# Second buffer for the gathered expert rows, passed on by ScalarE; scatter indices copied by VectorE; one TensorE wait per producer

## What is computed

```
x = x + L0_xattn(ctx_1024, layernorm(x))            # alignment, 8 x 100 rows of 512
h = layernorm(x)                                    # 800 rows
raw_gate = softmax(h @ gate)                        # 16 experts
_, topk_idx = top_k(raw_gate, 3)                    # TOP_K = int(16 * 0.2) = 3
gate_topk = normalised raw_gate of the 3 chosen
hidden = relu(h @ W1[e] + b1[e])                    # 512 -> 1024
expert_out = hidden @ W2[e] + b2[e]                 # 1024 -> 512
x = x + sum_e gate_topk[e] * expert_out[e]
x = x + L1_xattn(...);  x = x + L1_ffn(...)         # not touched by the change
```

## Time and profile before

| | |
|---|---|
| median of 3 runs | 1178.19 us (1177.99 to 1180.57) |
| the profiled execution: its own time | 1184.01 us |
| the profiled execution: span | 1181.7 us |
| TensorE (PE) busy in the span | 1042.0 us, 88% |
| GpSimd (POOL) busy in the span | 275.0 us, 23% |
| mean granted TensorE clock | 0.95 of full speed |

### The profile page before, as it was taken

The page is one execution under the profiler, slowest core; times in us unless marked ns, Lnnn a source line. Parts: engine busy times, 40 slices in busy tenths (PEclk is TensorE's granted clock), DMA queues, the critical chain, the costliest instruction groups (busy, mean ns, idle before and its releaser), DMA issues. The chain is left out here.

```text
span 1181.7 us, 19755 instructions
## 1 busy us (share of the span) xinstructions
PE 1042.0 (88%) x6297; PEld 642.8 (54%) x6298; DVE 520.6 (44%) x1963; ACT 327.8 (28%) x854; POOL 275.0 (23%) x416
## 2 busy tenths in 40 slices
PE   8967579956968998999989999889999999999997
PEld 7962235533455555555556555565456655555553
DVE  6837887884672222222222222237865643121212
ACT  4624755771121111111111111234254420000000
POOL 1852021110002333333333333410030001121211
PEclk9977889977988999999999999989999999999999
DMA  8857005118515574767677565570030005000000
GB/s 321 241 126 248 1 0 176 65 55 207 205 38 183 156 223 146 230 196 248 177 248 248 174 204 151 178 207 0 1 143 1 2 1 160 1 1 0 14 14 28
DMA packets 74653, 148.28 MB, mean 125 GB/s; under 512 B 12930, under 2 KB 24970, under 8 KB 73758
## 3 DMA queue, kind: packets, MB, share of 16 engines
q1 hardware_dynamic: 63750, 129.11, 33.0%
q0 software_dynamic: 9520, 14.56, 6.1%
q10 hardware_dynamic: 1320, 3.84, 1.3%
HBM read 128.16 MB, written 19.33 MB: 125 GB/s over the span
## 5 line engine op out<-in xcount | busy, mean ns | idle before, releaser
L1412 ACT ACTIVATE att<-ba,b 128x64 f32<-128x64 f32 x180 | 41.7, 314 | 232.9 <-PE ba L1335 232.9
L1318 PE MATMUL ba<-shared,att 128*64 128x256 f32 x736 | 91.2, 391 | 0.0
L2536 PE MATMUL acc<-tiles 128*128 128x400 f32 x256 | 90.6, 505 | 0.0
L2602 DVE SCALAR_TENSOR_TENSOR tiles<-bf,shared 128x400 f32<-128x400 f32 x64 | 32.4, 568 | 129.9 <-PE bf L2521 129.6
L1318 PE MATMUL ba<-Wmem,att 128*64 128x256 f32 x672 | 84.6, 395 | 1.0 <-ACT att L1397 0.5
L1343 PE MATMUL ba<-shared,att 128*64 128x256 f32 x736 | 84.6, 383 | 0.3 <-ACT att L1412 0.3
L1343 PE MATMUL ba<-Wmem,att 128*64 128x256 f32 x704 | 79.7, 379 | 0.0
L1432 DVE TENSOR_TENSOR att<-ba,att 128x256 f32<-128x256 f32 x45 | 19.1, 425 | 135.8 <-PE ba L1343 135.8
L2495 PE MATMUL bf<-shared,Wmem 128*128 128x400 f32 x192 | 70.0, 501 | 2.3 <-PEq L53 1.6
L2536 PEld LDWEIGHTS acc<-tiles 128*128 128x128 f32 x256 | 47.1, 190 | 40.4 <-issue 8.6
L1427 DVE TENSOR_SCALAR att<-ba,b 128x64 f32<-128x64 f32 x180 | 38.7, 277 | 68.6 <-PE ba L1335 68.5
(11 more groups left out here) (412 smaller groups left out, 1881.6 us busy)
## 6 DMA issues: line engine op xcount, KB each, us to landing
Wmem<-in_W SPq DMA_DIRECT2D x16, 2048.0 KB, 9.2
shared<-in_W SPq DMA_DIRECT2D x16, 2048.0 KB, 9.1
cT<-in_ctxT SPq DMA_DIRECT2D x8, 1444.0 KB, 14.7
ctx_rows<-in_ctx SPq DMA_DIRECT2D x8, 1280.0 KB
Wmem<-in_Wkv SPq DMA_DIRECT2D x2, 2048.0 KB, 8.3
tiles<-in_WoT SPq DMA_DIRECT2D x4, 1024.0 KB
Wmem<-in_WiT SPq DMA_DIRECT2D x3, 1024.0 KB, 6.9
cost_mem<-dist SPq DMA_DIRECT2D x8, 330.6 KB, 5.0
```

The lines of the kernel that those rows point to most:

```text
L1318: ins = pe.matmul(pa[part][h * Q:(h + 1) * Q, :], xT[:, k, :], w[:, k, h * HH + part * DQ:h * HH + (part + 1) * DQ], start=k == 0, stop=k ...
L1412: act.activation(hT[:, j, :], pt[0][:, n * P + half * Q:n * P + (half + 1) * Q], ACT.Relu, bias=b1[:, bass.ds((e + u) * HJ + j, 1)]).then_ ...
L2536: ins = pe.matmul(acc[k][:, 0:NT4], WoT[:, f, k * P:(k + 1) * P], hs[i % 4][:, :], start=f == 0, stop=f == FJ - 1)
L2602: dve.scalar_tensor_tensor((h1[i % 4], h2[i % 2])[k][:, :], bank[i % NBK][:, 0:NT4], 0.0, wb[k][:, g * NT4:(g + 1) * NT4], ALU.max, ALU.mu ...
```

## The change

`res["xg_sb"]` is a buffer for gathered rows with two halves in each of its slots. One more half, `ahead`, is now the target of every gather from the third on, and ScalarE copies it on to `rows` (`pass_on`) once it has landed in `ahead` and once the rows before have been turned; the copy raises `rows_ok`. GpSimd's `gather(c)` waits for `rows_ok` in place of TensorE's transposes, and TensorE waits for `rows_ok` in place of the transfer. The gather of the third chunk's rows is issued in the routing stage, behind the two that were there. The scatter's indices are copied by VectorE (in `output`, between its two operations, after the wait for the earlier scatter) and no longer by GpSimd. In TensorE's program several waits are gone: `turn_hidden` waits only for `a_rd[1]`, the second half of `first_layer` for nothing, and `second_layer` once for each of `h_ok[0]` and `h_ok[1]` (until all four relus of ScalarE, or of VectorE, are done) where it waited for each relu by itself. Waits at the end of the stage that counted gathers are gone too.

```diff
--- before.py
+++ after.py
@@ -1014,8 +1014,8 @@
 
             pool.wait_ge(idx_ok, 1)
             pool.wait_ge(kept_rows, 32 * B)
-            for i in range(2):
-                pool.indirect_dma_start(out=res["xg_sb"][:, i, 0:DQ], out_offset=None, in_=half_rows(res["xn_d"]),
+            for i, to in enumerate((res["xg_sb"][:, 0, 0:DQ], res["xg_sb"][:, 1, 0:DQ], res["xg_sb"][:, 0, DQ:D])):
+                pool.indirect_dma_start(out=to, out_offset=None, in_=half_rows(res["xn_d"]),
                                         in_offset=bass.IndirectOffsetOnAxis(ap=res["gidx"][:, i:i + 1], axis=0)).then_inc(res["xg_in"][i], 16)
 
         @block.tensor
@@ -1243,7 +1243,7 @@
     raw, y_last, y_more = pieces[:, 2, 0:DQ], pieces[:, 2, DQ:D], pieces[:, 3, 0:DQ]
     b2 = [pieces[:, 4, u * DQ:(u + 1) * DQ] for u in range(2)]
     xT = pieces[:, 5, 0:KD * Q].rearrange("p (k s) -> p k s", s=Q)
-    first_rows, rows = xg[:, 0, 0:DQ], xg[:, 1, 0:DQ]
+    first_rows, rows, ahead = xg[:, 0, 0:DQ], xg[:, 1, 0:DQ], xg[:, 0, DQ:D]
     from_row, to_more, to_last = (sb(n, [P, 1], I32) for n in ("from_row", "to_more", "to_last"))
     pa = [bank[0][:, 0:DQ], bank[1][:, 0:DQ]]
     pt, px, py = bank[2:4], bank[4][:, 0:DQ], bank[5][:, 0:DQ]
@@ -1251,9 +1251,10 @@
     w1_in, w2_in, xg_in = res["w1_in"], res["w2_in"], res["xg_in"]
     b1_in, x_back = sem("b1_in"), res["x_back"]
     a_mm, a_rd, h_ok = ([sem(f"{n}{i}") for i in range(2)] for n in ("a_mm", "a_rd", "h_ok"))
+    rows_ok = sem("rows_ok")
     xt_mm, xt_ok, t_mm, y_mm, py_rd, y_ok = (sem(n) for n in ("xt_mm", "xt_okd", "t_mm_e", "y_mm", "py_rd", "y_ok"))
     last_out, more_out, zeros = sem("last_out"), sem("more_out"), sem("zeros_e")
-    from_ok, to_ok = sem("from_ok"), sem("to_ok")
+    from_ok = sem("from_ok")
     took = sem("took_e")
     first_chunk = res["table"]
 
@@ -1312,7 +1313,8 @@
 
     def expert_pe(pe):
         def first_layer(c, w, part):
-            pe.wait_ge(a_rd[part], c)
+            if part == 0:
+                pe.wait_ge(a_rd[0], c)
             for k in range(KD):
                 for h in range(2):
                     ins = pe.matmul(pa[part][h * Q:(h + 1) * Q, :], xT[:, k, :], w[:, k, h * HH + part * DQ:h * HH + (part + 1) * DQ],
@@ -1325,10 +1327,7 @@
             ins.then_inc(xt_mm, 1)
 
         def turn_hidden(c):
-            for part in range(2):
-                pe.wait_ge(a_rd[part], c)
-            pe.wait_ge(h_ok[0], JH * c)
-            pe.wait_ge(h_ok[1], JH * c)
+            pe.wait_ge(a_rd[1], c)
             for i in range(2):
                 for n in range(2):
                     q = 2 * i + n
@@ -1338,7 +1337,8 @@
         def second_layer(c, w):
             pe.wait_ge(py_rd, c)
             for i, n, half, j in turned:
-                pe.wait_ge(h_ok[i], JH * c + 2 * n + half + 1)
+                if n == 0 and half == 0:
+                    pe.wait_ge(h_ok[i], JH * c)
                 for h in range(2):
                     ins = pe.matmul(py[h * Q:(h + 1) * Q, :], hT[:, j, :], w[:, j, h * DQ:(h + 1) * DQ],
                                     start=j == 0, stop=j == HJ - 1)
@@ -1348,7 +1348,7 @@
             pe.wait_ge(xt_ok, c + 1)
             first_layer(c, w1, 0)
             turn_hidden(c)
-            pe.wait_ge(xg_in[1], 16 * c + 16)
+            pe.wait_ge(rows_ok, c)
             turn_rows(rows)
             first_layer(c, w1, 1)
             second_layer(c, w2)
@@ -1383,9 +1383,9 @@
         pe.wait_ge(w2_in[1], 24 * (E_N - 2) + 48)
         with pe.Fori(c0 + 1, c1) as c:
             step(c, W1[1], W2[1])
+        pe.wait_ge(a_rd[0], c1)
         turn_hidden(c1)
         second_layer(c1, W2[1])
-        pe.wait_ge(xg_in[1], 16 * c1 + 16)
         pe.sem_inc(xt_mm, 1)
         pe.sem_inc(a_mm[0], 1)
         pe.sem_inc(a_mm[1], 1)
@@ -1396,12 +1396,16 @@
             act.wait_ge(a_mm[1], c + 1)
             act.copy(xT.rearrange("p (h m) s -> p m h s", h=2), px.rearrange("p (m h s) -> p m h s", m=2, h=2)).then_inc(xt_ok, 1)
 
-        act.sem_inc(h_ok[0], JH)
+        def pass_on(c):
+            act.wait_ge(xg_in[2], 16 * c + 16)
+            act.copy(rows, ahead).then_inc(rows_ok, 1)
+
         act.wait_ge(xt_mm, 1)
         act.copy(xT.rearrange("p (h m) s -> p m h s", h=2), px.rearrange("p (m h s) -> p m h s", m=2, h=2)).then_inc(xt_ok, 1)
         act.wait_ge(a_mm[0], 1)
         act.copy(pre[:, 0:DQ], pa[0]).then_inc(a_rd[0], 1)
         keep_rows(0)
+        pass_on(0)
         act.wait_ge(b1_in, 16)
         with act.Fori(0, E_N - 1, 2) as e:
             for u in range(2):
@@ -1415,6 +1419,7 @@
                     act.wait_ge(a_mm[0], c + 1)
                     act.copy(pre[:, 0:DQ], pa[0]).then_inc(a_rd[0], 1)
                     keep_rows(c)
+                    pass_on(c)
 
     def expert_dve(dve):
         def keep_second(c):
@@ -1427,15 +1432,16 @@
                 dve.tensor_scalar(hT[:, j, :], pt[1][:, n * P + half * Q:n * P + (half + 1) * Q], b1[:, bass.ds(e * HJ + j, 1)], 0.0,
                                   ALU.add, ALU.max).then_inc(h_ok[1], 1)
 
-        def output(c, u, y, y_out, before):
+        def output(c, u, y, to_row, y_out, before):
             dve.wait_ge(y_mm, c)
             dve.tensor_tensor(raw, py, b2[u], ALU.add).then_inc(py_rd, 1)
+            dve.wait_ge(y_out, before)
+            dve.sem_inc(took, 1)
+            dve.tensor_copy(to_row[:, :], res["oidx"][:, bass.ds(c - 1, 1)])
             dve.wait_ge(py_rd, c + 1)
-            dve.wait_ge(y_out, before)
             dve.tensor_scalar(y, raw, res["gate_s"][:, bass.ds(c - 1, 1)], None, ALU.mult).then_inc(y_ok, 1)
 
         dve.sem_inc(py_rd, 1)
-        dve.sem_inc(h_ok[1], JH)
         kb = res["kbias"]
         dve.tensor_scalar(kb[:, :, 0:KC], res["fill"][:, :, :], -BIG, BIG, ALU.mult, ALU.add)
         dve.memset(kb[:, :, KC:NK], 0.0)
@@ -1448,33 +1454,28 @@
                 with dve.Fori(m0 + 1, m1 + 1) as m:
                     hidden(m + e + u, e + u)
                     keep_second(m + e + u)
-                    output(m + e + u, u, y_more, more_out, 16 * m)
+                    output(m + e + u, u, y_more, to_more, more_out, 16 * m)
                 hidden(m1 + e + u + 1, e + u)
                 keep_second(m1 + e + u + 1)
-                output(m1 + e + u + 1, u, y_last, last_out, 16 * e + 16 * u + 16)
+                output(m1 + e + u + 1, u, y_last, to_last, last_out, 16 * e + 16 * u + 16)
 
     def expert_pool(pool):
         def gather(c):
-            pool.wait_ge(xt_mm, c + 2)
+            pool.wait_ge(rows_ok, c)
             pool.tensor_copy(from_row[:, :], res["gidx"][:, bass.ds(c + 2, 1)]).then_inc(from_ok, 1)
             pool.wait_ge(from_ok, c)
             pool.sem_inc(took, 1)
-            pool.indirect_dma_start(out=rows, out_offset=None, in_=half_rows(res["xn_d"]),
-                                    in_offset=bass.IndirectOffsetOnAxis(ap=from_row[:, 0:1], axis=0)).then_inc(xg_in[1], 16)
+            pool.indirect_dma_start(out=ahead, out_offset=None, in_=half_rows(res["xn_d"]),
+                                    in_offset=bass.IndirectOffsetOnAxis(ap=from_row[:, 0:1], axis=0)).then_inc(xg_in[2], 16)
 
         def scatter(c, y, to_row, y_out):
             pool.wait_ge(y_ok, c)
-            pool.tensor_copy(to_row[:, :], res["oidx"][:, bass.ds(c - 1, 1)]).then_inc(to_ok, 1)
-            pool.wait_ge(to_ok, c)
             pool.sem_inc(took, 1)
             pool.indirect_dma_start(out=half_rows(res["sum_d"]), out_offset=bass.IndirectOffsetOnAxis(ap=to_row[:, 0:1], axis=0),
                                     in_=y, in_offset=None, compute_op=ALU.add).then_inc(y_out, 16)
 
         for y in (y_more, y_last):
             pool.memset(y, 0.0).then_inc(zeros, 1)
-        pool.wait_ge(xt_mm, 2)
-        pool.indirect_dma_start(out=rows, out_offset=None, in_=half_rows(res["xn_d"]),
-                                in_offset=bass.IndirectOffsetOnAxis(ap=res["gidx"][:, 2:3], axis=0)).then_inc(xg_in[1], 16)
         pool.wait_ge(zeros, 2)
         for i, (y, y_out) in enumerate(((y_more, more_out), (y_last, last_out))):
             pool.dma_start(half_rows(res["sum_d"])[2 * XT + i * P:2 * XT + (i + 1) * P, :], y).then_inc(y_out, 16)
@@ -1489,9 +1490,6 @@
                     scatter(m + e + u, y_more, to_more, more_out)
                 gather(m1 + e + u + 1)
                 scatter(m1 + e + u + 1, y_last, to_last, last_out)
-        every = pool.value_load(first_chunk[0:1, E_N:E_N + 1], min_val=2 * E_N, max_val=CHUNKS)
-        pool.wait_ge(xg_in[1], 16 * every + 32)
-        pool.sem_inc(took, 1)
 
     return last_out, expert_sp, expert_pe, expert_act, expert_pool, expert_dve
```

## The result

| | before | after |
|---|---|---|
| median | 1178.1 us | 1162.8 us (1162.24 to 1163.88, 4 runs) |
| profiled execution: its own time; its span | 1184.01 us; 1181.7 us | 1162.24 us; 1160.5 us |

The ratio of after to before is 0.987, 95% interval 0.985 to 0.9891; later, on another chip, it was 0.990 (0.9864 to 0.9937). The change is faster by about 15 us. The forecast was 1186.1 us, slower by 7.9; the result lies near the first rival, 1167.

A forecast was written before the change was run, and what follows sets the result against it. TensorE's idle was taken as the bound: 35.8 us in 25 waits for gathers, held by scatters and weights. Terms 4.5 + 5.0 - 1.9 + 0.0 + 0.3 = +7.9 on 1178.19 gave 1186.1 us, range 1166 to 1191.

The forecast's parts named there:

- rival 1: The first rival: last-chunk gathers issued beside `W1` get ahead of the weights, seven waits go; 1167 us, chance 0.20.
- Case B: Also B: nine waits for the gather of an expert's last chunk, beside `W1`; 0.55 us more each, +5.0 us.
- the full hop: The whole 0.55 us of ScalarE's added copy, charged to each of nine last-chunk gathers beside `W1`: +5.0 us.
- The hop: ScalarE's copy of landed rows before TensorE may use them: 0.55 us per late gather, bounds 0.4 to 0.75.
- Case A: 15 waits for the gather behind the scatter of an expert's last chunk, beside `W2`; 0.30 later each, +4.5 us.
- The third gather: Issued in the routing stage, it removes the first step's idle of 1.67 and 0.21 us: -1.9 us.
- Fewer waits: Dropping TensorE's waits gains 0; at most 0.1 us in each of 45 chunks, -4.5 us.
- The end: At the end TensorE's second layer waits for four relus, +0.6, and the last scatter gives back 0.25: +0.3 us.
- Rival 2: ScalarE's added copy and the earlier scatter cancel, or TensorE gains from fewer waits: about 1179 us, chance 0.12.
- the low bound of the hop: ScalarE's added copy costs only 0.4 us per late gather, if the semaphore costs nothing.
- the third rival: Everything is hidden: all 35.8 us of gather waits and the 1.67 go; 1141 us, chance 0.05.

The follow-up runs named there:

- index copy alone: The kernel before, with VectorE copying the scatter indices, no second buffer, TensorE's waits as they were: 1164.0 us, 0.9884.
- buffer alone: The kernel before, with the second buffer, ScalarE's copy and the third gather in routing; GpSimd still copies the scatter indices: 1186.3 us, 1.0077.
- best kernel: The changed kernel, with GpSimd's order turned so that the gather for the next chunk but one stands ahead of the scatter: 1136.1 us, 0.9648.
- `W1` behind the gather: The kernel before, with SyncE issuing `W1` only when the gather under way has landed: 1151.1 us, 0.9725.
- index copy and `W1` later: The kernel before, with VectorE copying the scatter indices and SyncE issuing `W1` after VectorE's copy of the sums: 1152.0 us, 0.9737.
- the same order with one buffer: The kernel before (one buffer, GpSimd copies scatter indices), with GpSimd's order turned to put the gather ahead of the scatter: 1155.4 us, 0.9817.

## Why the prediction was wrong

**The bound and the cause were right.** The waits ahead of `turn_rows` are what the time moved with, and B was the company of `W1` (its wait is gone where `W1` comes after the gather). So was the second buffer's uselessness behind a scatter: alone it cost 9 us.

**The step that failed** is "Case B: I take the full hop", +5.0, and the chance of 0.20 given to rival 1. The nine waits went from 19.6 to 5.5 us, -14.1. The race was seen, but all three of its numbers were off.

- *The start.* The 0.26 behind `W1` was read from one row and taken for all seven. It is the smallest of the seven; the others stood 0.49 to 1.18 behind. With that read, the prediction's own sum would have been still surer of a lost race.
- *The shift.* It was put at 0.25 + 0.55 = 0.80 and came to 0.96 for this gather and 1.28 on average. The index copy alone moved the leads by 0.81 and not 0.25, since it counts twice, in the last chunk's scatter and in the scatter that waits for its landing; the buffer alone moved them by 0.28 and not 0.55.
- *What is needed.* It was put at 0.90 to 1.0 from a low in the DMA rates, as if all of the gather's data had to be ahead of the weights. TensorE wants the rows only some 5.4 us after the issue, and for that a lead of 0.47 was enough: 0.73 for the gather of the earlier trace rows, up to 1.65 for the others.

So rival 1 named the right mechanism, but that its 1167 came near the result is in part luck, since the start and the shift were wrong in opposite directions. And a margin of 0.1 to 0.2 in a race whose stake is 19 us can't bear a chance of only 0.20: the terms themselves were not known to 0.1 us. Where the race was lost, the forecast of "the full hop" did not hold either: the buffer alone lengthened the nine waits by 0.24 each, not 0.55.

**The hop**: by the gather's semaphore in the trace, TensorE starts 0.48 after the landing (503.03 to 503.51) and before 0.04 (516.77 to 516.81), so it costs 0.44, against 0.55; right in kind. **Case A**: +3.4 us measured, +4.5 forecast. The terms as named, 0.55 - 0.25, were mis-sized both ways. Alone, the hop costs 0.38 each, and the earlier scatter gives 0.12 each, not 0.25, because the landing goes by `W2`.

**The third gather**: 1.67 and 0.21 are gone, as forecast, -1.9. **Fewer waits**: 0, as forecast. **The end**: 1.1 us for ScalarE's relus, 0.5 before, as forecast.

**Two slips** changed nothing above. ScalarE's 0.37, cited from the earlier trace rows, stands in the earlier trace rows. Rival 2 takes 0.1 us off 24 gathers for the low bound of the hop, which is 0.15 below 0.55; its time is then 1178 and not 1179.

**A term was missing.** The waits account for 12.6 of the stage's 15.1 us (37.5 to 24.9), and for 37.5 of the 44.6 us of the best kernel. The rest goes with TensorE's clock. Windows of the kernel before, around's last wait (columns: window, its length, busy time of PE, PEld, DVE, ACT, POOL, then the granted clock, DMA share, GB/s):

```profile
708.20:711.60 3.40, 2.18 (x20) 1.20 (x16) 1.55 (x6) 1.19 (x5) 1.49 (x2) 1.00 1.01 386
...
712.80:716.20 3.40, 3.40 (x20) 1.95 (x18) 0.34 (x1) 0.29 (x1) 1.08 (x2) 0.50 0.26 44
716.20:719.60 3.40, 3.40 (x36) 2.26 (x34) 0.12 (x2) 0.09 (x1) 0.00 (x0) 1.00 0.13 39
```

TensorE stood idle for 1.91 us up to 712.06, and from 712.80 its clock was 0.50, the level of 1.2 GHz, for 3.4 us, with 20 matmuls done where the next stretch has 36. The whole stage has a granted clock of 0.97 before, 0.98 after and 0.99 in the best kernel:

```profile
361.00:755.20 394.20, 361.30 (x3066) 229.53 (x3066) 91.58 (x308) 69.39 (x266) 129.99 (x177) 0.97 0.66 203
```

```profile
354.40:733.50 379.10, 356.96 (x3066) 228.52 (x3066) 94.48 (x351) 85.81 (x305) 121.90 (x133) 0.98 0.67 211
```

```profile
365.20:714.80 349.60, 348.00 (x3066) 226.47 (x3067) 93.62 (x347) 82.53 (x305) 121.78 (x134) 0.99 0.73 227
```

With the same 3066 matmuls, PE is busy for 361.3, 357.0 and 348.0 us. Across the runs, the stage less its waits for gathers goes by the number of such slow stretches in it, besides one at its start that all have: 349.4 to 349.7 us in the three with none and little else to wait for ("`W1` behind the gather", "index copy and `W1` later", the best kernel), 354.3 in the changed kernel with three, 356.8 in the kernel before with five, so some 1.5 us each. That long waits bring them is read from where they stand: in the kernel before, five of the seven waits of 1.9 us or more have one with them, those of 2.22 and 1.94 us have none. No run held the waits and changed the clock alone.

**The rule on double buffering** of the Trainium skill ("Trainium Kernel Development and Optimization", Best Practices) stood beside the third rival, which had 0.05 and gave 1141. It did not hold for the change and did for the change with the gather first, 1136: a second buffer hides a transfer once its issue is free of what it was to be hidden from.

## What to carry to other kernels

A transfer into a second buffer starts no earlier than its place in the issuing engine's program: move the issue ahead of what waits for the end of the step, or the buffer only adds a hop. Where a small transfer and a large one start within a microsecond of each other, read where each of them starts in every turn and not in one, compute the race with both shifts, give the outcome a chance that fits the error of the terms, and look for the one wait that decides it without a race, here one line at SyncE. Allow for slower clock behind long idles of TensorE.

## What the hardware showed that was not expected

The race between a gather of 128 KB and a weight load of 2 MB is not all or nothing: within half a microsecond of lead the landing moves by some 3.5 us. Two gathers of the changed kernel that were in time, issued at 547.78 and 572.31 with leads of 0.47 and 0.76, were passed on as soon as they had landed, 5.20 and 3.28 us after their issue:

```profile
552.98 0.41 ACT L1401 COPY xg_sb<-xg_sb 128x256 f32<-128x256 f32 x1 [4.45 <-DMA xg_sb<-xn_d,from_row]
...
575.59 0.40 ACT L1401 COPY xg_sb<-xg_sb 128x256 f32<-128x256 f32 x1 [2.23 <-DMA xg_sb<-xn_d,from_row]
```

By the gathers' semaphores in the traces of the runs above, in experts with three or more chunks, one landed 2.6 to 2.9 us after its issue with a lead of 0.88 to 0.92 ("the same order with one buffer"), which is about what one in the kernel before took with no weights beside it (2.7 to 3.2); 4.4 to 4.9 with 0.55 to 0.60, and 6.2 us or more with 0.21 to 0.40. That the waits went all at once comes from TensorE, which wants the rows some 5.4 us after the issue. The Trainium skill, "DMA: Bandwidth & Descriptors", Queues, rings and completion order, says that a DMA engine takes turns between queues packet by packet. By that rule alone a gather of 1/16 of the bytes would lose little wherever it started. The trace does not agree: a gather issued 0.26 behind `W1` was used 6.79 us after its issue. No run here shows why it loses as much as it does.

GpSimd's start of an indirect transfer took 0.80 us behind the last wait, whether an index copy and its semaphore stood ahead of it or VectorE's output released it directly: a copy taken off GpSimd gave the whole of its 0.18 and its handshake, 0.36 together (1.16 to 0.80).
